# Last cross attention: the mask's bias added by VectorE for 15 of 49 pairs of key tiles

## The chip, the cores and the metric

One Trainium2 chip, one core. The metric is the device time of one execution in microseconds (us), lower is better; several runs are taken and their median is given.

## What is computed

The program is a twelve-stage network (four rounds of cross attention, self attention and feed-forward) over 128 rows of 256 features, `x`, with a context of 12544 rows of 256, `ctx_1024`. The change is in the tenth stage, the last cross attention, whose reference is this:

```python
def _L3_xattn_ref(queries, keys, values, mask):     # N_HEADS = 16
    q, k, v = heads(queries), heads(keys), heads(values)          # 16 features per head
    sim = jnp.einsum('bhqd,bhkd->bhqk', q, k) / jnp.sqrt(jnp.float32(d_head))
    bias = -1000000000.0 * (1.0 - mask.astype(sim.dtype))[:, None]
    sim = sim + bias
    weights = jax.nn.softmax(sim, axis=-1)
    out = jnp.einsum('bhqk,bhkd->bhqd', weights, v)

x = x + _L3_xattn_ref(_layernorm(x), ctx_1024, ctx_1024, mask_BxSxS2_ik1)
```

The mask has 128 x 12544 integers, 0 or 1, and is the same for all heads.

## The kernel before

`stage_l3_xattn` has 16 heads in 8 groups of two. The 12544 keys are 98 tiles of 128; two tiles are one pair, so that a group has 49 pairs and the stage 392. `SEGS` cuts the work into ten segments: group 0 in three (7, 14 and 28 pairs, so that work can begin early), each other group in one of 49. The masks' bias, `NEG` times (mask - 1), lies in SBUF for all keys as `key_bias`, rows of queries by columns of keys.

For each segment there are two passes. The first finds a maximum: TensorE multiplies queries by keys into one of two double banks `ps_s` (`scores`, L1648, two matmuls of 448 columns for a unit of 896 keys and one head), and VectorE adds the bias and reduces (`largest`, L1795). GpSimd turns the maximum of a segment into three parts that are put into the matrix of queries (`largest` of GpSimd, L1748 to L1755, which signals `m`); TensorE transposes it (`queries`, L1655), and VectorE copies it to `qb`. The second pass takes each pair of tiles with keys on the partitions (`tiles`, L1664 and L1666): for each tile a product of `key_bias` with an identity, `eye`, which lays the turned bias into PSUM, and the product of the keys with `qb`, added to it. A pair fills one of three banks `ps_t` (four tiles of 128 x 128: two tiles by two heads). ScalarE takes the exponential of the whole bank into `p` (L1727), a ring of eight. TensorE multiplies values by it (`values`, L1678).

The order on TensorE is written out: phases of four or five pairs; in each the tiles of the phase, with the scores for the next segment placed between them (`placed`: 28 units of scores and maxima over some 42 pairs, two in three pairs; none for the last group), then the values of the phase before. VectorE runs the maxima in the same order. `wait_slot` lets the tiles of a pair wait until the bank's earlier user is done, which is the exponential three pairs before, or a query or turn between. `scores` waits for the maximum two units before.

At the stage's start GpSimd clears buffers, copies the first values (`copy(0)`, L1760) and takes the first maximum (`largest(0)`). SP issues the first two loads of values, and the keys of group 1 once ScalarE has filled a buffer with ones (`k_ones`, L1722).

The core of the tiles:

```python
pe.matmul(ps_t[b][:, h * 2 * T:(h + 1) * 2 * T], bias[:, t * T:(t + 1) * T],
          eye[:, :, :].rearrange("p a t -> p (a t)"), start=True, stop=False)
mm = pe.matmul(ps_t[b][:, h * 2 * T:(h + 1) * 2 * T], kst[g % 2][:, t * T:(t + 1) * T],
               qb[:, i % 2, :, :].rearrange("p a t -> p (a t)"), start=False, stop=True)
```

Of the kernel before, what the change touches and what calls it, by code (L numbers as in the profile page):

```python
# [11 lines left out]
ALU = mybir.AluOpType  # L12
# [6 lines left out]
T = 128  # L19
# [4 lines left out]
CT = CH // 128  # L24
HALF = CH // 2
NCH = S2 // CH
ARENA = 52100
FAR = -2.0 ** 100
NEG = 954.0 * 2 ** 20
AHEAD = S2  # L30
# [1489 lines left out]
def stage_l3_xattn(nc, A, x, ident):  # L1520
# [21 lines left out]
    for i, n in enumerate(size):  # L1542
        parts = max(1, round(n / 4))
        for j in range(parts):
            phases.append((i, range(first[i] + j * n // parts, first[i] + (j + 1) * n // parts), j == parts - 1))
    fast = P * 2 * T + 2 * 2 * T + 2 * T
    with Stage(nc, "l3x", fast=fast, held=HELD) as s:
        kst, bias = A["kst"], A["key_bias"]
        qs, qb = s.sb("qs", [128, P, 2, T], F32R), s.sb("qb", [128, 2, 2, T], F32R)
# [8 lines left out]
        wide = flat("wide", P * 128).rearrange("p (g a r b) -> p g a r b", g=P, a=2, r=16)  # L1558
        v_in = flat("v_in", 2 * SEG * 32).rearrange("p (j t a e) -> p j t a e", j=2, t=SEG, a=2)
        v = flat("v", 2 * SEG * 64).rearrange("p (j t a e) -> p j t a e", j=2, t=SEG, a=2)  # L1560
        p = flat("p", R * 4 * T).rearrange("p (r j a t) -> p r j a t", r=R, j=2, a=2)
        junk = s.sb("junk", [128, 2, CH])
        qh = junk[:, 0, 0:D]
        far, negm, rest = s.sb("far", [128, 1]), s.sb("negm", [128, 2, 2]), s.sb("rest", [128, 2, 2])
# [32 lines left out]
        @block.sync  # L1597
        def _(sp):
            def keys(g, seg):
                j, lo = g % 2, seg * SEG * T  # L1600
                if g == 1:
                    sp.wait_ge(s.sem("k_ones"), seg // 4 + 1)
                for part, b in (("ctx_high", 0), ("ctx_low", 1), ("ctx_high", 2)):
                    sp.dma_start(kst[j][b:128:4, lo:lo + SEG * T].bitcast(F32),
                                 A[part][32 * g:32 * g + 32, lo:lo + SEG * T]).then_inc(s.sem(f"k_in{j}{seg}"), 16)

            def values(q):
                g, seg = divmod(q, NS)
                wait(sp, "v", q - 1)
                sp.dma_start(v_in[:, q % 2, :, :, :].rearrange("p t a e -> p (t a e)"),  # L1610
                             A["ctx_pairs"][:, g, seg * SEG * 32:(seg + 1) * SEG * 32]).then_inc(s.sem(f"v_in{q % 2}"), 16)

            values(0)
            values(1)
            for seg in range(NS):
                keys(1, seg)
            for q in range(P * NS):
                if q + 2 < P * NS:
                    values(q + 2)
                if q < (P - 2) * NS:  # L1620
                    wait(sp, "tiles", (q + 1) * 7)
                    keys(q // NS + 2, q % NS)

        @block.tensor
        def _(pe):
# [32 lines left out]
            def tiles(i, u):  # L1658
                g, b = SEGS[i][0], slot["tiles", u]
                wait_slot(pe, ("tiles", u))  # L1660
                pe.wait_ge(s.sem("qb"), 2 * i + 2)
                for h in range(2):
                    t = 2 * (u % 49) + h
                    pe.matmul(ps_t[b][:, h * 2 * T:(h + 1) * 2 * T], bias[:, t * T:(t + 1) * T],  # L1664
                              eye[:, :, :].rearrange("p a t -> p (a t)"), start=True, stop=False)
                    mm = pe.matmul(ps_t[b][:, h * 2 * T:(h + 1) * 2 * T], kst[g % 2][:, t * T:(t + 1) * T],  # L1666
                                   qb[:, i % 2, :, :].rearrange("p a t -> p (a t)"), start=False, stop=True)
                mm.then_inc(s.sem("tiles"), 1)

            def values(i, u):  # L1670
                pe.wait_ge(s.sem("v"), u // 7 + 1)
                pe.wait_ge(s.sem("p"), u + 1)
                if u == first[i]:
                    wait(pe, "outT", i)
                for h in range(2):
                    for a in range(2):
                        c = 2 * h + a
                        mm = pe.matmul(ps_o[32 * c:32 * c + 32, 0:T], v[:, u // 7 % 2, u % 7 * 2 + h, a, :], p[:, u % R, h, a, :],  # L1678
                                       start=(u == first[i]), stop=(u == first[i + 1] - 1))
                mm.then_inc(s.sem("values"), 1)  # L1680

# [28 lines left out]
        def _(act):  # L1710
# [12 lines left out]
            for i, groups, ends in phases:  # L1723
                for u in groups:
                    act.wait_ge(s.sem("tiles"), u + 1)
                    wait(act, "values", u - R + 1)
                    act.activation(p[:, u % R, :, :, :].rearrange("p h a t -> p (h a t)"), ps_t[slot["tiles", u]][:, :],  # L1727
                                   ACT.Exp).then_inc(s.sem("p"), 1)
                if accs[i] == 3 and groups[0] == first[i]:
                    act.wait_ge(s.sem("diff"), i)  # L1730
# [3 lines left out]
        def _(pool):  # L1734
# [22 lines left out]
            def copy(q):  # L1757
                pool.wait_ge(s.sem(f"v_in{q % 2}"), (q // 2 + 1) * 16)
                wait(pool, "values", (q - 1) * 7)
                pool.tensor_copy(v[:, q % 2, :, :, 0:16], v_in[:, q % 2, :, :, :]).then_inc(s.sem("v"), 1)  # L1760

            pool.wait_ge(s.sem("v_ones"), 2)
            copy(0)
            pool.wait_ge(s.sem("wide"), 1)
# [9 lines left out]
        def _(dve):  # L1774
# [32 lines left out]
            def turn(i):  # L1807
# [12 lines left out]
                dve.wait_ge(s.sem("acc"), done + accs[i] - 1)  # L1820
                dve.tensor_tensor(mine, mine, parts[:, 1, :, :], ALU.add).then_inc(s.sem("acc"), 1)

            def out(i):
                dve.wait_ge(s.sem("values"), first[i + 1])
                wait(dve, "out_ps", i)
# [5 lines left out]
            due, last = None, None  # L1831
            for i, groups, ends in phases:
                for u in groups:
                    for k in placed.get(u, []):
                        largest(k)
                if ends and i + 1 < len(SEGS):
# [1660 lines left out]
def more_layouts(i, out):  # L3497
# [11 lines left out]
    out["mask_bk1"] = i["mask_BxS2_bk1"][0].astype(np.int32)  # L3509
    out["mask_ff1"] = i["mask_BxS2_ff1"][0].reshape(-1, 128).T  # L3510
    out["mask_ik1"] = i["mask_BxSxS2_ik1"][0]
    out["L2_xattn_wq"] = chunked(i["L2_xattn_wq"])
    out["L2_xattn_wkv"] = chunked(np.concatenate([i["L2_xattn_wk"], i["L2_xattn_wv"]], 1))
    out["L2_xattn_dense_w"] = chunked(i["L2_xattn_dense_w"])
# [139 lines left out]
```

## Time and profile before

| | |
|---|---|
| median of 3 runs | 2784.79 us (2784.68 to 2785.99) |
| the profiled execution | 2784.39 us, its span 2782.7 us |
| mean granted TensorE clock | 0.949 |
| busy over the span | TensorE 2548.3 us (92%), VectorE 1637.7 (59%), ScalarE 1419.1 (51%), GpSimd 650.8 (23%) |
| the stage of the change | about 2272 to 2710 us |

The span is the time from the first to the last instruction of the profiled execution. A row of the time line has the start, the duration, the engine, the line of the code, the operation, what it writes and reads, a count of merged instructions, and in brackets how long the engine was idle before and what released it. A row of the groups has line, engine, operation, names, shapes and count, then busy time and mean of one, then the idle time before it. PE is TensorE, DVE VectorE, ACT ScalarE, POOL GpSimd, SPq the queue of SyncE. Matmuls overlap, so that their cost is the distance of their starts.

### The profile page before, as it was taken

The page shows a single profiled execution, that of the slowest core. Times are in us where ns is not written, and L with a number is a line of the kernel's source. Part 1 is how long each engine was busy: PE and PEld are TensorE (multiplying, and loading weights), DVE is VectorE, ACT ScalarE, POOL GpSimd, SP SyncE. Part 2 cuts the span into 40 slices and gives each one's busy share as a digit, 9 for nine tenths or more (in the row PEclk, how much of TensorE's full clock was granted, in tenths as well). Part 3 has the DMA queues.
Part 4 walks back from the last instruction along what each step waited for, and adds up shares of the span by engine and source line. Part 5 has one row for each costly group of instructions (what it writes and reads, how often), then busy time and mean ns, then how long its engine had stood idle before and what let it go on. Part 6 is the DMA issues. An engine that isn't in the chain of part 4 may idle for free. (4 is left out here: it accounts for less than half of the span.)

```text
span 2782.7 us, 67701 instructions
## 1 busy us (share of the span) xinstructions
PE 2548.3 (92%) x25738; PEld 2122.6 (76%) x25738; DVE 1637.7 (59%) x4181; ACT 1419.1 (51%) x2670; POOL 650.8 (23%) x888
## 2 busy tenths in 40 slices
PE   8999999999999999997859999999976359999986
PEld 6888888888888888886857888888842127888873
DVE  5667556656665566656684555555552337666625
ACT  5555555555555555553645555565520433555553
POOL 1323132313231323112014554545100000101000
PEclk9999999999999999999889999999987679999996
DMA  4011101111011101100831111112058654344310
GB/s 166 15 55 41 54 15 55 41 54 39 30 41 55 54 15 44 39 15 24 306 124 67 68 68 68 39 63 72 2 218 294 258 196 134 121 134 134 104 39 34
DMA packets 67194, 236.07 MB, mean 85 GB/s; under 512 B 12924, under 2 KB 22944, under 8 KB 60640
## 3 DMA queue, kind: packets, MB, share of 16 engines
q1 hardware_dynamic: 64208, 218.43, 22.6%
q0 software_dynamic: 2304, 8.39, 0.9%
q8 instruction: 214, 3.51, 0.5%
q10 hardware_dynamic: 368, 4.92, 0.4%
q14 instruction: 100, 0.82, 0.1%
HBM read 205.65 MB, written 26.05 MB: 83 GB/s over the span
## 5 line engine op out<-in xcount | busy, mean ns | idle before, releaser
L469 PE MATMUL l0x_psum<-l0x_fast 128*128 128x512 f32 x1764 | 432.0, 397 | 2.8 <-ACT l0x_sbuf L593 1.3
L469 PEld LDWEIGHTS l0x_psum<-l0x_fast 128*128 128x128 f32 x1764 | 323.8, 189 | 67.4 <-ACT l0x_sbuf L593 1.7
L604 ACT ACTIVATE l0x_sbuf<-l0x_sbuf 128x896 f32<-128x896 f32 x224 | 233.3, 1041 | 237.0 <-DVE l0x_sbuf L718 237.0
L1727 ACT ACTIVATE l3x_sbuf<-l3x_psum 128x512 f32<-128x512 f32 x392 | 220.9, 599 | 187.8 <-PE l3x_psum L1666 181.2
L1795 DVE CUSTOM_DVE_ANT_0 l3x_sbuf<-l3x_psum,key_bias,l3x_sbuf 128x896 f32<-128x896 f32 x224 | 249.0, 1149 | 93.3 <-PE l3x_psum L1648 76.8
L449 PE MATMUL l0x_psum<-l0x_fast 128*128 128x448 f32 x1344 | 292.5, 367 | 1.1 <-DVE l0x_fast L704 1.1
L449 PEld LDWEIGHTS l0x_psum<-l0x_fast 128*128 128x128 f32 x1344 | 252.0, 188 | 26.0 <-DVE l0x_fast L704 1.5
L718 DVE CUSTOM_DVE_ANT_0 l0x_sbuf<-l0x_psum,l0x_sbuf 128x896 f32<-128x896 f32 x224 | 249.1, 1150 | 20.6 <-PE l0x_psum L484 20.6
L855 POOL TENSOR_TENSOR l0x_sbuf<-l0x_sbuf 128x2 f32<-128x2 f32 x112 | 31.2, 278 | 890.6 <-ACT l0x_sbuf L621 890.6
L704 DVE TENSOR_TENSOR l0x_fast<-l0x_psum,l0x_fast 128x448 fp32r<-128x448 f32 x224 | 136.3, 616 | 129.3 <-ACT l0x_fast L579 129.3
L1664 PE MATMUL l3x_psum<-l3x_fast,key_bias 128*128 128x256 f32 x784 | 208.2, 296 | 0.7 <-DVE l3x_fast L1805 0.7
L579 ACT ACTIVATE l0x_fast<-l0x_psum 128x448 fp32r<-128x448 f32 x224 | 120.4, 544 | 166.3 <-PE l0x_psum L449 166.2
L1666 PE MATMUL l3x_psum<-l3x_fast,last_keys 128*128 128x256 f32 x784 | 197.1, 281 | 0.0
L529 PE MATMUL l0x_psum<-l0x_sbuf 128*32 128x128 f32 x6272 | 195.9, 274 | 1.2 <-DVE l0x_sbuf L757 1.2
L529 PEld LDWEIGHTS l0x_psum<-l0x_sbuf 128*32 128x32 f32 x6272 | 165.9, 109 | 35.1 <-issue 33.6
L704 DVE TENSOR_TENSOR l1x_fast<-l1x_psum,l1x_fast 128x448 fp32r<-128x448 f32 (+1 forms) x116 | 69.9, 612 | 207.6 <-ACT l1x_fast L579 207.3
L604 ACT ACTIVATE l1x_sbuf<-l1x_sbuf 128x896 f32<-128x896 f32 (+1 forms) x120 | 119.6, 996 | 115.1 <-DVE l1x_sbuf L718 115.1
L593 ACT ACTIVATE l0x_sbuf<-l0x_psum 128x512 f32<-128x512 f32 x196 | 117.6, 601 | 109.2 <-PE l0x_psum L469 109.2
L484 PE MATMUL l0x_psum<-l0x_fast 64*128 64x448 f32 x1344 | 167.3, 381 | 0.0
L1664 PEld LDWEIGHTS l3x_psum<-l3x_fast,key_bias 128*128 128x128 f32 x784 | 148.5, 189 | 22.6 <-issue 14.9
L966 DVE BATCH_NORM_STATS2 l0x_sbuf<-l0x_sbuf 128x6 f32<-128x256 f32 x98 | 42.0, 428 | 205.5 <-ACT l0x_sbuf L941 205.5
L741 DVE COPY l0x_sbuf<-l0x_psum 128x384 f32<-128x384 f32 x224 | 125.1, 559 | 59.1 <-PE l0x_psum L536 40.3
(767 smaller groups left out, 5153.0 us busy)
## 6 DMA issues: line engine op xcount, KB each, us to landing
ahead<-in_L_ffn_W SPq DMA_DIRECT2D x22, 1024.0 KB, 14.6
last_keys<-ctx_high SPq DMA_DIRECT2D x98, 224.0 KB, 3.5
l0x_sbuf<-in_ctxT SPq DMA_DIRECT2D x14, 896.0 KB, 6.1
l0x_sbuf<-in_ctx_rows SPq DMA_DIRECT2D x14, 896.0 KB, 4.4
ctx_high<-l0x_fast SPq DMA_DIRECT2D x14, 896.0 KB, 8.6
ctx_low<-l0x_fast SPq DMA_DIRECT2D x14, 896.0 KB, 10.2
soon<-in_ctxT SPq DMA_DIRECT2D x14, 896.0 KB, 5.0
l3x_sbuf<-in_ctx_pairs SPq DMA_DIRECT2D x56, 224.0 KB, 3.7
```

Source lines behind the costliest of these rows:

```text
L449: mm = pe.matmul(ps[:, 0:width], self.wk[w][:, c, pr * T:(pr + 1) * T], x[:, c, lo:lo + width], start=(j == 0), stop=(j == len(products) - 1))
L469: mm = pe.matmul(ps[:, :], x[:, c, t * T:(t + 1) * T], weights[w][:, c, :], start=(j == 0), stop=(j == len(products) - 1))
L484: mm = pe.matmul(self.ps_s[a][:, i, 0:width], self.q[q][half, pr, :], self.k[k][half, m % 2, lo:lo + width], start=(j == 0), stop=(j == 2))
L529: mm = pe.matmul(self.ps_o[32 * c:32 * c + 32, :], self.v[:, m // 4 % 2, t, at:at + 32], self.pT[:, (2 * m + c // 2) % 4, t, :], start=(t ...
L604: act.activation(self.p[:, (2 * m + a) % 4, 0:width], self.sm[:, a, 0:width], ACT.Exp, scale=-1.0, bias=self.negm[:, n % 2, 2 * pr + a:2 * ...
L704: dve.tensor_tensor(self.k[1][:, m % 2, lo:lo + width], self.ps_kv[self.slot["k", m, i]][:, 0:width], self.k[0][:, m % 2, lo:lo + width].b ...
L718: dve.tensor_tensor_reduce(self.sm[:, a, 0:parts * width].rearrange("p (i c) -> p i c", i=parts), self.ps_s[a][:, 0:parts, 0:width], bias. ...
L741: dve.tensor_copy(self.pT[:, i % 4, 4:CT, :], cols(self.turned_banks(m, a)[1], CT - 4)).then_inc(s.sem(f"ptb{a}"), 1)
L1664: pe.matmul(ps_t[b][:, h * 2 * T:(h + 1) * 2 * T], bias[:, t * T:(t + 1) * T], eye[:, :, :].rearrange("p a t -> p (a t)"), start=True, sto ...
L1666: mm = pe.matmul(ps_t[b][:, h * 2 * T:(h + 1) * 2 * T], kst[g % 2][:, t * T:(t + 1) * T], qb[:, i % 2, :, :].rearrange("p a t -> p (a t)") ...
L1727: act.activation(p[:, u % R, :, :, :].rearrange("p h a t -> p (h a t)"), ps_t[slot["tiles", u]][:, :], ACT.Exp).then_inc(s.sem("p"), 1)
L1795: dve.tensor_tensor_reduce(junk[:, a, :].rearrange("p (i c) -> p i c", i=2), ps_s[a][:, :, 0:HALF], bias[:, n * CH:(n + 1) * CH].bitcast(F ...
```

## The change

Of the 49 pairs of a group, the 15 with numbers 2, 5, 8, ..., 44 are masked on VectorE in all eight groups, 120 pairs in all. For these TensorE leaves out the two products with the identity; VectorE adds `-NEG * outside` to the bank in PSUM (one SCALAR_TENSOR_TENSOR over 128 x 512, in place), where `outside` is 1 - mask as bytes with keys on the partitions, the same bytes for both heads. ScalarE waits for it before the exponential. The host hands in the turned mask of these pairs as integers (`mask_turned`, 128 x 15 x 2 x 128, 1.97 MB). SP loads it into the space of `p`, and GpSimd turns it into bytes before its first copy. The order inside a bank and inside a slot of `p` changes from tile, head to head, tile, so that one broadcast serves both heads.

```diff
-ARENA = 52100
+ARENA = 52148
+    apart = {u: i for i, u in enumerate(range(2, 47, 3))}
+    set_apart = [u for u in range(P * 49) if u % 49 in apart]
+    masked = {u: i + 1 for i, u in enumerate(set_apart)}
-        p = flat("p", R * 4 * T).rearrange("p (r j a t) -> p r j a t", r=R, j=2, a=2)
+        p = flat("p", R * 4 * T).rearrange("p (r a j t) -> p r a j t", r=R, a=2, j=2)
+        outside = s.sb("outside", [128, len(apart) * 2 * T // 4], I32).bitcast(mybir.dt.uint8).rearrange(
+            "p (u h t) -> p u h t", u=len(apart), h=2)
+        raw = p[:, :, :, :, :].rearrange("p r a j t -> p (r a j t)").bitcast(I32)[:, 0:len(apart) * 2 * T].rearrange(
+            "p (u h t) -> p u h t", u=len(apart), h=2)
             values(1)
+            sp.dma_start(raw, A["mask_turned"]).then_inc(s.sem("turned_in"), 16)
             for seg in range(NS):
...
                     t = 2 * (u % 49) + h
-                    pe.matmul(ps_t[b][:, h * 2 * T:(h + 1) * 2 * T], bias[:, t * T:(t + 1) * T],
-                              eye[:, :, :].rearrange("p a t -> p (a t)"), start=True, stop=False)
-                    mm = pe.matmul(ps_t[b][:, h * 2 * T:(h + 1) * 2 * T], kst[g % 2][:, t * T:(t + 1) * T],
-                                   qb[:, i % 2, :, :].rearrange("p a t -> p (a t)"), start=False, stop=True)
+                    both = ps_t[b][:, :].rearrange("p (a h t) -> p a h t", a=2, h=2)[:, :, h, :]
+                    if u not in masked:
+                        pe.matmul(both, bias[:, t * T:(t + 1) * T],
+                                  eye[:, :, :], start=True, stop=False)
+                    mm = pe.matmul(both, kst[g % 2][:, t * T:(t + 1) * T], qb[:, i % 2, :, :], start=u in masked, stop=True)
...
                     wait(act, "values", u - R + 1)
+                    if u == 0:
+                        act.wait_ge(s.sem("outside"), 1)
+                    if u in masked:
+                        act.wait_ge(s.sem("masked"), masked[u])
...
+            pool.wait_ge(s.sem("turned_in"), 16)
+            pool.tensor_scalar(outside, raw, -1.0, 1.0, ALU.mult, ALU.add).then_inc(s.sem("outside"), 1)
             pool.wait_ge(s.sem("v_ones"), 2)
             copy(0)
...
+            def mask(u):
+                dve.wait_ge(s.sem("outside"), 1)
+                dve.wait_ge(s.sem("tiles"), u + 1)
+                both = ps_t[slot["tiles", u]][:, :].rearrange("p (a k) -> p a k", a=2)
+                dve.scalar_tensor_tensor(out=both, in0=outside[:, apart[u % 49], :, :].rearrange("p h t -> p (h t)").unsqueeze(1).to_broadcast([128, 2, 2 * T]),
+                                         scalar=-NEG, in1=both, op0=ALU.mult, op1=ALU.add).then_inc(s.sem("masked"), 1)
...
                 for u in groups:
+                    if u in masked:
+                        mask(u)
                     for k in placed.get(u, []):
                         largest(k)
```

## Rows read from the trace of the kernel before

**Rows 1.** Stretches of the stage: busy time by engine, granted clock, DMA share, GB/s.

```profile
core 0: us, PE busy (x) PEld busy (x) DVE busy (x) ACT busy (x) POOL busy (x), PEclk, DMA share, GB/s
...
2292.00:2305.30 13.30, 10.47 (x69) 8.36 (x69) 9.23 (x18) 7.37 (x9) 1.60 (x7) 0.88 0.95 329
2305.30:2329.70 24.40, 21.07 (x202) 17.63 (x202) 18.64 (x37) 8.36 (x15) 2.17 (x8) 0.92 0.34 114
2329.70:2370.00 40.30, 37.71 (x402) 30.99 (x398) 31.94 (x62) 16.76 (x29) 2.67 (x8) 0.97 0.29 91
...
2419.40:2468.70 49.30, 49.30 (x650) 43.50 (x646) 32.65 (x61) 27.73 (x50) 4.68 (x12) 1.00 0.43 132
...
2666.20:2705.50 39.30, 39.26 (x633) 35.19 (x629) 0.74 (x3) 25.61 (x50) 3.75 (x7) 1.00 0.12 32
```

**Rows 2.** Groups of instructions of the stage, 2292 to 2706 us.

```profile
L1795 DVE CUSTOM_DVE_ANT_0 l3x_sbuf<-l3x_psum,key_bias,l3x_sbuf 128x896 f32<-128x896 f32 x220 | 244.6, 1149 | 88.1 <-PE l3x_psum L1648 71.6 <-issue 16.5
...
L1664 PE MATMUL l3x_psum<-l3x_fast,key_bias 128*128 128x256 f32 x784 | 208.2, 296 | 0.7 <-DVE l3x_fast L1805 0.7
...
L1648 PE MATMUL l3x_psum<-last_keys,l3x_fast 128*128 128x448 f32 x440 | 128.4, 376 | 3.2 <-DVE l3x_sbuf L1795 3.1
```

**Rows 3.** Time line inside a full round, all engines.

```profile
2400.22 0.57 PE L1648 MATMUL l3x_psum<-last_keys,l3x_fast 128*128 128x448 f32 x2
2400.42 0.60 ACT L1727 ACTIVATE l3x_sbuf<-l3x_psum 128x512 f32<-128x512 f32 x1 [1.46 <-PE l3x_psum L1666]
...
2400.62 0.28 PE L1664 MATMUL l3x_psum<-l3x_fast,key_bias 128*128 128x256 f32 x1
...
2400.83 1.15 DVE L1795 CUSTOM_DVE_ANT_0 l3x_sbuf<-l3x_psum,key_bias,l3x_sbuf 128x896 f32<-128x896 f32 x1 [0.92 <-PE l3x_psum L1648]
...
2401.09 0.28 PE L1664 MATMUL l3x_psum<-l3x_fast,key_bias 128*128 128x256 f32 x1
...
2402.44 0.57 PE L1648 MATMUL l3x_psum<-last_keys,l3x_fast 128*128 128x448 f32 x2
...
2402.94 1.08 PE L1678 MATMUL l3x_psum<-l3x_sbuf 128*32 128x128 f32 x32
...
2403.95 0.38 PE L1664 MATMUL l3x_psum<-l3x_fast,key_bias 128*128 128x256 f32 x1
...
2404.17 0.28 PE L1666 MATMUL l3x_psum<-l3x_fast,last_keys 128*128 128x256 f32 x1
```

**Rows 4.** Time line of maxima and scores among pairs 21 to 48.

```profile
2348.95 1.15 DVE L1795 CUSTOM_DVE_ANT_0 l3x_sbuf<-l3x_psum,key_bias,l3x_sbuf 128x896 f32<-128x896 f32 x1 [0.78 <-PE l3x_psum L1648]
...
2350.03 1.15 DVE L1795 CUSTOM_DVE_ANT_0 l3x_sbuf<-l3x_psum,key_bias,l3x_sbuf 128x896 f32<-128x896 f32 x1
...
2350.26 0.65 PE L1648 MATMUL l3x_psum<-last_keys,l3x_fast 128*128 128x448 f32 x2
```

**Rows 5.** Time line at the end of a round: ScalarE's exponentials, TensorE's next tile.

```profile
2416.43 2.07 ACT L1727 ACTIVATE l3x_sbuf<-l3x_psum 128x512 f32<-128x512 f32 x4 [1.04 <-PE l3x_psum L1666]
...
2417.17 0.30 PE L1664 MATMUL l3x_psum<-l3x_fast,key_bias 128*128 128x256 f32 x1
```

**Rows 6.** Groups of VectorE over the whole span, shapes kept apart.

```profile
L3077 DVE SCALAR_TENSOR_TENSOR l0f_sbuf<-l0f_sbuf,l0f_psum 128x512 f32<-128x512 f32 x16 | 10.4, 685 | 21.9 <-ACT l0f_sbuf L3044 21.9
```

**Rows 7.** Time line of the stage's start: SP and GpSimd.

```profile
2272.33 0.80 SPq L1610 DMA_DIRECT2D l3x_sbuf<-in_ctx_pairs  x2
...
2277.55 0.56 POOL L1760 COPY l3x_sbuf<-l3x_sbuf 128x448 f32<-128x448 f32 x1
...
2289.47 0.19 POOL L1748 CAST l3x_sbuf<-l3x_sbuf 128x2 fp32r<-128x2 f32 x1 [11.37 <-DVE l3x_sbuf L1795]
...
2289.65 0.49 SPq L1604 DMA_DIRECT2D last_keys<-ctx_high  x1
```

**Rows 8.** Groups of GpSimd over the whole span, shapes kept apart.

```profile
L828 POOL TENSOR_SCALAR l1x_sbuf<-l1x_sbuf 128x896 f32<-128x896 int32 x14 | 45.2, 3226 | 29.4 <-DMA l1x_sbuf<-in_mask_bk 28.3
...
L809 POOL TENSOR_SCALAR soon<-soon,l1x_sbuf 128x896 f32<-128x896 f32 x26 | 28.4, 1092 | 2.7
```

More of the change, by code:

```diff
@@ L1677, in values @@
                         c = 2 * h + a
-                        mm = pe.matmul(ps_o[32 * c:32 * c + 32, 0:T], v[:, u // 7 % 2, u % 7 * 2 + h, a, :], p[:, u % R, h, a, :],
+                        mm = pe.matmul(ps_o[32 * c:32 * c + 32, 0:T], v[:, u // 7 % 2, u % 7 * 2 + h, a, :], p[:, u % R, a, h, :],
                                        start=(u == first[i]), stop=(u == first[i + 1] - 1))
@@ L1726, in _ @@
                     wait(act, "values", u - R + 1)
-                    act.activation(p[:, u % R, :, :, :].rearrange("p h a t -> p (h a t)"), ps_t[slot["tiles", u]][:, :],
+                    if u == 0:
+                        act.wait_ge(s.sem("outside"), 1)
+                    if u in masked:
+                        act.wait_ge(s.sem("masked"), masked[u])
+                    act.activation(p[:, u % R, :, :, :].rearrange("p a h t -> p (a h t)"), ps_t[slot["tiles", u]][:, :],
                                    ACT.Exp).then_inc(s.sem("p"), 1)
@@ L3511, in more_layouts @@
     out["mask_ik1"] = i["mask_BxSxS2_ik1"][0]
+    out["mask_turned"] = i["mask_BxSxS2_ik1"][0].T.reshape(49, 2, 128, T)[2:47:3].transpose(2, 0, 1, 3)
     out["L2_xattn_wq"] = chunked(i["L2_xattn_wq"])
```

## The prediction

> **What bounds the kernel now.** I read the stage of the last cross attention by stretches first [rows 1]. Its columns give, for each stretch, the busy time of every engine and the granted clock. From 2370 us on the 392 pairs of key tiles run in rounds of 49 pairs. A full round (2419.40 to 2468.70) has TensorE busy all 49.30 us at clock 1.00, VectorE 32.65 and ScalarE 27.73. So TensorE sets the pace of the six rounds that also compute scores for the next one, and of the last round (39.26 of 39.30 us, VectorE only 0.74). The first 49 pairs are different: TensorE 10.47 of 13.30, 21.07 of 24.40 and 37.71 of 40.30 us, clock 0.88 to 0.97. There scores and maxima come more densely, and the stage starts.
>
> Next the groups of the stage [rows 2]. The product with the identity, L1664, runs 784 times, two for each pair. Its mean of 296 ns is latency, since matmuls overlap. What a matmul costs must be read from the distance of starts [rows 3]: two score matmuls (one "S") take 2400.22 to 2400.62, 0.40 us. A pair has four tile matmuls; 2400.62 to 2401.09 are four of them, so T = 0.47 us, 0.117 each. A pair without identity is T' = 0.23 us. After a phase of four pairs come the 32 value matmuls "V": 2402.94 to 2403.95, and with 0.10 ahead of it 1.11 us. The first tile matmul after V takes 0.22 in place of 0.12 (2403.95 to 2404.17).
>
> **The sum for TensorE alone.** Twelve pairs (three phases) have 8 S: 12 x 0.47 + 8 x 0.40 + 3 x (1.11 + 0.10) = 12.5 us. A round of 49 pairs in 49.3 us fits that. The change takes out 2 x 120 = 240 of these matmuls, 30 per round: 30 x 0.117 = 3.5 us per round, 28 in all. That is the most it can bring. From 12.5 a cycle of twelve pairs would fall to 11.6.
>
> **The new path.** In a masked pair ScalarE's exp no longer follows the product directly. VectorE must add the bias first, in its own order, behind the maxima that it has queued. Behind the waiting mask stand the next maxima (L1795) and so TensorE's next scores. Behind the exp that waits stand all later exps. A pair uses one of three PSUM banks, so the tiles of pair u+3 wait for the exp of pair u.
>
> The prices. A maximum occupies VectorE for 1.15 us, but the next starts 1.07 to 1.08 later [rows 2, 4]. A first maximum starts 0.61 after its S starts (2400.22 to 2400.83), an exp 0.20 after the last tile matmul has been issued (2400.22 to 2400.42) [rows 3]. S waits for the maximum two before it, plus 0.23 (2350.03 to 2350.26) [rows 4]. Exp runs 0.60 us, back to back every 0.49, and TensorE goes on 0.14 after the end of it (2416.43 + 0.60 to 2417.17) [rows 3, 5]. For the mask M no row writes PSUM from VectorE. The nearest is a SCALAR_TENSOR_TENSOR of 128x512 with one operand in PSUM, 685 ns [rows 6]. I take M = 0.68. The lower bound is one element at the pace of the 896-element maximum, 512/896 x 1.15 = 0.66; the upper one is the whole price of that maximum, 1.15. Bytes as input I price like fp32. With 0.1 from VectorE to ScalarE the bank of a masked pair is free 0.84 us after M ends.
>
> **One cycle by hand**, time 0 at the first tile after V. TensorE: T0 0, S0 0.57, T1, S1 1.44, T2' ends 2.07, T3, S3 2.54, V, T4 4.05, S4 4.62, T5', T6, S6 5.72, T7, S7 6.59, V, T8' 8.10, T9, S9 8.91, T10, S10 9.78, T11' 10.18, V, end 11.52. VectorE: maxima 1.18, 2.25; M2 3.32 to 4.00; maxima 4.00, 5.23; M5 6.30 to 6.98; maxima 6.98, 8.05; M8 9.12 to 9.80; maxima 9.80, 10.87; M11 11.94 to 12.62; the next may start at 12.70. VectorE's sum is 8 x 1.07 + 4 x 0.68 = 11.3 of 11.5 us, so it just keeps up and is always late by about a maximum. Which banks are late? Pair 6 needs exp 3, which queued behind exp 2: 0.08. Pair 11 needs the bank of pair 8: 9.80 + 0.84 = 10.64 against 10.18: 0.46. The others are in time, mostly because V stands between. A cycle gains 0.93 - 0.54 = 0.39.
>
> The rest of a round: pairs 36 to 39 gain 0.23. In the last nine pairs two masks save 0.47, but pair 44 waits 0.52 for the mask of 41, and pair 47 waits for 44 with only two pairs between them: 0.21 + 0.68 + 0.84 = 1.73 less 2 x 0.47 is 0.79. That is 0.84 lost. A round gains 3 x 0.39 + 0.23 - 0.84 = 0.56, six rounds 3.4 us. In the last round 15 x 0.23 = 3.5 are saved and four times 0.79 lost (8 to 11, 20 to 23, 32 to 35, 44 to 47): 0.3.
>
> **The first 49 pairs.** Pairs 0 to 6 run eight maxima without a gap, then GpSimd takes the result. M2 stands among them: +0.7; M5 comes after them and is hidden. Pairs 7 to 20 have 16 maxima and VectorE 18.64 of 24.40 us busy [rows 1]; four masks are 2.7 us, and V's gaps can take some 1.5 of it: +1.2. In pairs 21 to 48 each V leaves a gap of 0.78 in front of a maximum [rows 4]. One mask fits in, and eight masks meet seven phases, one of them saved matmuls too: +0.3. Together +2.2, bounds 0.5 and 8 (no cover for twelve of the masks).
>
> **The start.** GpSimd now waits for 1.97 MB of mask, turns it to bytes, and only then does copy and `largest(0)`, for which the first `m`, the queries, every tile and every maximum wait. Before, that chain began at 2289.47, its cover since the copy of 2277.55 [rows 7]. The issue follows the two at 2272.33, so at 2273.1. At 329 GB/s with the DMA 0.95 busy [rows 1], 1.97 MB take 6 us; with 0.45 MB ahead and some 1.5 us to land, about 2281.4. Then the pass of 3840 integers a partition. The nearest row is a TENSOR_SCALAR from int32 on GpSimd: 896 elements in 3226 ns [rows 8], 3.5 ns each above 0.1, so 13.4 us. The same instruction on fp32 takes 1092 ns, which would be 4.7 us. The integer row shares the input type, so I take it: end 2294.8, copy 0.6, `largest(0)` at 2295.5 in place of 2289.5: +6.0. Nothing takes this back, since the first pairs are VectorE's. Bounds 0 and 10. The added DMA issue on SP stands ahead of the loads of the next keys, which wait for ScalarE's fill until 2289.65 anyway [rows 7]: nothing. The layout of `p` and of the PSUM bank leaves all counts and sizes as they were: nothing, bounds -1 and +1.
>
> The Trainium skill speaks against my price for the pass: "GPSIMD Engine Reference", section 4.1 Engine selection, says that one-input elementwise work on GpSimd is roughly at line rate. By it the pass would be hidden (first rival). The fp32 row agrees with it, the int32 row does not.
>
> **Sum.** +6.0 + 2.2 - 3.4 - 0.3 = +4.5 us on the profiled execution's 2784.39 (span 2782.7 and 1.7 around it), which is 0.4 under the median of 2784.79: 2789.3. A measurement here tells about 0.2% (5.6 us) from no change, so this lies just inside "same".
>
> **Rivals.**
> 1. Quick bytes: the pass runs at the fp32 row's 1.2 ns, is done by 2286 and hidden. Time 2783. For it the fp32 row, against it the int32 row, 14 times alike. Its rule is the one of the page named above.
> 2. Masks hidden: VectorE's real lateness is smaller than I drew, because its handover is shorter or the order slips into V. Then most of 3.5 us per round stays: half of it gives 2784.4 + 6 + 2 - 14 = 2778, all of it 2766. For it: TensorE has no slack today and VectorE has 16 us idle per round. Against it: two pairs between 44 and 47, 8 and 11.
> 3. VectorE becomes the bound (slower). Place: the cycle of twelve pairs. It decides from M = (12.5 - 8.6)/4 = 0.98 us on; writing PSUM or reading bytes would have to cost 0.3 more than the 685 ns row. At 0.98 a cycle gains nothing and the tails lose 0.3 more for each late bank: 2784.4 + 6 + 5 + 6 x 1.5 + 1.5 = 2806; at 1.15 about 2820.
> 4. Bytes out cost extra on GpSimd: 5 ns per element, 19 us, start +12: 2795. No row writes bytes, so nothing excludes it.
> 5. The change does not do what it says (the identity products stay): 2790.
>
> **Chances.** Forecast 0.45 (own range 2784 to 2795), rival 1 0.15, 2 0.13, 3 0.13, 4 0.12, 5 0.02. Faster: rival 2, and 0.02 each of the forecast and rival 1, 0.17. Slower (above 2790.4): 0.17 of the forecast, rivals 3 and 4, 0.42. Within: the rest, 0.41. The range for 8 in 10 leaves out the far ends of rivals 2 and 3: 2779 to 2804.
>
> **What will show it.** L1664 has 544 matmuls. GpSimd's TENSOR_SCALAR to uint8 x1 lasts 13.4 us (4.7: rival 1; 19: rival 4), and the cast of `largest(0)` starts near 2295.5. The masks x120 show 0.68 us. A full round takes 48.8 us; TensorE has gaps of some 0.5 before pair 11 and 0.8 before pair 47 of a round, released by ScalarE. If a round takes 46 to 47 us, rival 2 holds; if VectorE is busy throughout and a round exceeds 50, rival 3. The clock stays 1.00 in the rounds; a lower one there would make the prediction wrong in a way that I have not priced.

## The result and the profile after

The changed kernel takes 2790.3 us (median of 20 runs, 2783.15 to 2795.76), the kernel before 2786.05 in the same runs. The ratio is 1.0019, with a 95% interval of 1.0012 to 1.0026: 5 us slower (3 to 7), within the 0.2% that the prediction called "same". The forecast was 2789.3.

The profiled execution took 2785.99 us (span 2784.2), one of the quicker ones. Executions of one and the same code differ by a few us, so the change is read from the stage alone, and there from its parts. The table cuts the stage at the start of the first load on SP, at the first cast of each set of queries on VectorE, and at the first load of the next stage. All numbers are us from the traces; the kernels below the second row are the experiments of the next section.

| kernel | start | pairs 0-6 | 7-20 | 21-48 | a full round | six rounds | last round | stage |
|---|---|---|---|---|---|---|---|---|
| before | 18.96 | 13.28 | 24.40 | 40.36 | 49.36 | 295.94 | 44.71 | 437.65 |
| after | 18.67 | 13.88 | 25.40 | 41.59 | 49.05 | 294.20 | 47.49 | 441.23 |
| setup_only | 18.67 | 13.40 | 23.56 | 39.02 | 49.54 | 297.03 | 44.64 | 436.32 |
| layout_only | 18.95 | 13.28 | 24.23 | 39.85 | 49.36 | 295.95 | 44.69 | 436.95 |
| no_add | 18.67 | 13.70 | 24.83 | 38.57 | 46.07 | 276.18 | 43.02 | 414.97 |
| both | 18.66 | 13.93 | 25.60 | 41.85 | 51.43 | 308.32 | 49.30 | 457.66 |
| first_only | 18.67 | 14.15 | 25.07 | 41.73 | 49.54 | 297.03 | 44.64 | 441.29 |
| rounds_only | 18.67 | 13.28 | 24.24 | 39.82 | 49.05 | 294.10 | 44.64 | 434.75 |
| one_a_phase | 18.67 | 13.28 | 24.22 | 39.82 | 48.30 | 289.59 | 44.65 | 430.23 |
| no_tail | 18.67 | 13.73 | 23.73 | 40.71 | 48.20 | 288.98 | 44.65 | 430.47 |
| without_5 | 18.67 | 13.43 | 23.57 | 39.01 | 48.51 | 291.08 | 44.62 | 430.38 |
| best | 18.66 | 13.28 | 24.30 | 39.94 | 47.73 | 286.17 | 43.94 | 426.29 |

The six rounds of a trace repeat within 0.1 us, save the first, which is some 0.2 us shorter in most traces ("a full round" is one of the other five). The first 49 pairs vary from kernel to kernel: seven other kernels mask nothing there, and with before they take 76.0 to 78.2 us for the same work.

Stretches of after, the columns as in [rows 1]: the three segments of the first 49 pairs, a full round, and 12.5 us of the last round (some fifteen pairs).

```profile
2289.45:2303.36 13.91, 10.29 (x65) 8.17 (x66) 10.45 (x20) 7.35 (x9) 1.61 (x7) 0.87 0.96 331
2303.36:2328.76 25.40, 20.30 (x188) 16.11 (x188) 21.52 (x42) 7.92 (x15) 2.18 (x8) 0.90 0.31 105
2328.76:2370.30 41.54, 35.77 (x390) 28.93 (x384) 36.61 (x70) 15.86 (x29) 2.69 (x8) 0.98 0.28 84
2418.50:2467.50 49.00, 47.70 (x620) 40.27 (x620) 41.13 (x76) 25.96 (x50) 4.82 (x11) 1.00 0.43 133
...
2676.30:2688.80 12.50, 11.88 (x181) 9.80 (x180) 3.48 (x5) 8.57 (x16) 1.14 (x2) 1.00 0.14 39
```

In a full round VectorE rose from 32.65 to 41.13 us, TensorE is no longer busy throughout (47.70 of 49.00), and the clock stayed at 1.00. In the last round TensorE has gaps too. In the first 49 pairs VectorE is busy 85 to 88% of the second and third segment.

The groups of the stage in after: the mask on VectorE, the identity product, the exponential.

```profile
L1842 DVE SCALAR_TENSOR_TENSOR l3x_psum<-l3x_sbuf,l3x_psum 128x512 f32<-128x512 uint8 x120 | 83.2, 693 | 33.7 <-PE l3x_psum L1676 33.1
...
L1674 PE MATMUL l3x_psum<-l3x_fast,key_bias 128*128 128x256 f32 x544 | 151.8, 303 | 3.7 <-ACT l3x_sbuf L1740 3.0
...
L1740 ACT ACTIVATE l3x_sbuf<-l3x_psum 128x512 f32<-128x512 f32 x392 | 210.1, 599 | 202.5 <-DVE l3x_psum L1842 149.9
```

The change does what it says: 544 identity products in place of 784, 120 masks at 693 ns. The exponential's idle time is now mostly ended by the mask.

And the start of the stage, time line of SP and GpSimd.

```profile
2270.08 0.81 SPq L1617 DMA_DIRECT2D l3x_sbuf<-in_ctx_pairs  x2
2270.93 0.42 SPq L1622 DMA_DIRECT2D l3x_sbuf<-in_mask_turned  x1
...
2280.59 3.39 POOL L1776 TENSOR_SCALAR l3x_sbuf<-l3x_sbuf 128x3840 uint8<-128x3840 int32 x1 [5.36 <-DMA l3x_sbuf<-in_mask_turned]
...
2286.93 0.19 POOL L1761 CAST l3x_sbuf<-l3x_sbuf 128x2 fp32r<-128x2 f32 x1 [2.43 <-DVE l3x_sbuf L1810]
```

The load lands 9.6 us after its issue, the pass takes 3.39 us and not 13.4, and GpSimd waits another 2.43 us for VectorE before the cast of `largest(0)`, 16.85 us after the first issue of the stage (2270.08). In the trace of before it is 17.14 [rows 7]. So the start costs nothing.

### The profile page after: what moved, and what is told of

Read it like the earlier page. It is cut to its first block and busy times, and to the rows that moved or that the text cites. A ratio compares the mean times of both kernels' runs of the same rounds, so it can differ in the third digit from the quotient of the medians.

```text
span 2784.2 us, 67470 instructions
## 1 busy us (share of the span) xinstructions
PE 2526.9 (91%) x25498; PEld 2088.9 (75%) x25498; DVE 1713.8 (62%) x4301; ACT 1408.4 (51%) x2670; POOL 655.5 (24%) x889
## 3 DMA queue, kind: packets, MB, share of 16 engines
q8 instruction: 212, 3.47, 0.5%
## 5 line engine op out<-in xcount | busy, mean ns | idle before, releaser
L1740 ACT ACTIVATE l3x_sbuf<-l3x_psum 128x512 f32<-128x512 f32 x392 | 210.1, 599 | 202.5 <-DVE l3x_psum L1842 149.9
L1676 PE MATMUL l3x_psum<-l3x_fast,last_keys 128*128 128x256 f32 x784 | 191.0, 290 | 4.0 <-ACT l3x_sbuf L1740 3.6
L1676 PEld LDWEIGHTS l3x_psum<-l3x_fast,last_keys 128*128 128x128 f32 x784 | 143.5, 190 | 20.1 <-ACT l3x_sbuf L1740 14.6
L1674 PE MATMUL l3x_psum<-l3x_fast,key_bias 128*128 128x256 f32 x544 | 151.8, 303 | 3.7 <-ACT l3x_sbuf L1740 3.0
```

The lines of the kernel that those rows point to most:

```text
L1674: pe.matmul(both, bias[:, t * T:(t + 1) * T], eye[:, :, :], start=True, stop=False)
L1676: mm = pe.matmul(both, kst[g % 2][:, t * T:(t + 1) * T], qb[:, i % 2, :, :], start=u in masked, stop=True)
L1740: act.activation(p[:, u % R, :, :, :].rearrange("p a h t -> p (a h t)"), ps_t[slot["tiles", u]][:, :], ACT.Exp).then_inc(s.sem("p"), 1)
```

## The experiments

The theory to begin with was the prediction's, less its start: TensorE's saving is full where it sets the pace, and is eaten by PSUM banks that the mask's detour over VectorE frees late. Rivals were that the loss comes from the load, the layout or the larger stage; that TensorE would not have gained in the first place; and, for cures, that the number of masks counts and not their place.

**setup_only**: the load, the bytes and the layout, no pair masked.

```diff
-    set_apart = [u for u in range(P * 49) if u % 49 in apart]
+    set_apart = []
```

> The mask is loaded and turned to bytes at the stage's start, the new layout is used, but no pair is masked on VectorE: all identity products stay. Prediction's step (the pass costs 13.4 us and delays the first tiles by 6.0): time before + 6, so ratio 1.002. First rival (the pass takes 3.4 us as the trace of after shows, and lies in GpSimd's wait): time before, ratio 1.000, first cast of the queries 18.7 to 19.0 us after the stage's first load is issued, rounds of 49.36 us.

Measured: 2784.26 us, ratio 0.9995 (0.9986 to 1.0004); start 18.67 us. The prediction's +6.0 falls, the first rival's picture of the start holds. The full rounds are 49.54 us, 0.18 longer than in before, which neither expected.

**layout_only**: the kernel before, with the order of bank and slot changed.

```diff
...
+                    both = ps_t[b][:, :].rearrange("p (a h t) -> p a h t", a=2, h=2)[:, :, h, :]
-                    pe.matmul(ps_t[b][:, h * 2 * T:(h + 1) * 2 * T], bias[:, t * T:(t + 1) * T],
-                              eye[:, :, :].rearrange("p a t -> p (a t)"), start=True, stop=False)
+                    pe.matmul(both, bias[:, t * T:(t + 1) * T], eye[:, :, :], start=True, stop=False)
...
```

> The kernel before with only the order inside bank and slot changed (head, tile in place of tile, head): no load, no bytes, no mask. setup_only showed rounds of 49.54 in place of 49.36 us. If the layout costs this, rounds are 49.54 here; if the load, the larger stage or the bytes do, 49.36.

Measured: rounds of 49.36 us, one run of 2786.62. The layout costs nothing: TensorE writes two stretches of 128 columns, 256 apart, as quickly as 256 in a row. The Trainium skill, "PSUM — Partial Sum Buffer", Specifications, says that any non-contiguous pattern slows matmuls significantly; for stretches this long the measurement says no. The 0.18 of setup_only must then come from the rest of the set-up: the load, the bytes, the waits that go with them or the 48 words by which the stages' arena grew; which one was not tried. It is no single wait: from one group of value products to the next setup_only takes 4.33, 4.32 and 3.91 us in a cycle of twelve pairs, layout_only 4.30, 4.30 and 3.92.

**no_add**: the saving alone. VectorE's addition and ScalarE's wait for it are left out, so that the masked keys of these pairs are counted in.

```diff
-                    if u in masked:
-                        act.wait_ge(s.sem("masked"), masked[u])
...
-                    if u in masked:
-                        mask(u)
```

> The identity products of the 120 pairs are left out and VectorE adds nothing, so that the masked keys of these pairs are counted in: what is left is TensorE's saving alone. If the handover through VectorE is what eats the gain (prediction), the six full rounds fall by 3.3 to 3.5 us each, 20 us together; the first 49 pairs stay, since maxima set their pace (0 to 2 us). For the last round two theories: by the prediction's sum it falls by 3.5 us; if three banks and the exponential bound its phases (a bank is free 0.9 us after its tile, two tiles are 0.94), only masked pairs at the first or last place of a phase save, about 2 us. Total: 22 to 25 us under before, ratio 0.992. If TensorE had not been the bound: ratio 1.000.

Measured: 2759.75 us, ratio 0.9906 (0.9891 to 0.9921). Against setup_only a full round falls by 3.47 us (49.54 to 46.07), which is all of 30 x 0.117 = 3.5. The last round falls by 1.62 only: the theory of three banks and the exponential said 2, the prediction's sum 3.5. The first 49 pairs take 77.1 us, no less than without the change: VectorE's maxima set their pace.

**both**: the detour alone. The 120 pairs keep their identity products and are masked by VectorE as well.

```diff
-                    if u not in masked:
+                    if True:
...
-                    mm = pe.matmul(both, kst[g % 2][:, t * T:(t + 1) * T], qb[:, i % 2, :, :], start=u in masked, stop=True)
+                    mm = pe.matmul(both, kst[g % 2][:, t * T:(t + 1) * T], qb[:, i % 2, :, :], start=False, stop=True)
```

> The 120 pairs keep their identity product and get VectorE's addition as well (the masked scores are lowered twice, which leaves their exponential at zero): the handover alone. Prediction: full rounds of 12 pairs rise from 12.5 by some 0.3, the last nine pairs of a round by 1.3 to 1.5, so a round is 51 to 51.5 us; the last round gains 4 to 6 us; the first 49 pairs rise by 3 to 4. Total 15 to 22 us over before, ratio 1.006 to 1.008. Rival (the wait is hidden and the loss in after has another source, such as the load or the layout): ratio under 1.002.

Measured: 2806.93 us, ratio 1.0077 (1.0063 to 1.0091). Against setup_only a round rises by 1.9, the last round by 4.7, the first 49 pairs by 5.4 (by 4.2 against the mean of the kernels without masks there). The detour is dear by itself, and saving and detour do not simply add up: per round -3.47 + 1.89 is -1.6, while after shows -0.49. The likely reading of the other 1.1 us is saving that turns into waiting, since with shorter tiles TensorE reaches a late bank sooner; the gaps below show such waits.

**first_only**: the masks of group 0 alone.

```diff
-    set_apart = [u for u in range(P * 49) if u % 49 in apart]
+    set_apart = [u for u in range(49) if u % 49 in apart]
```

> Only the 15 masked pairs of group 0 (the first 49 pairs) go over VectorE, all others keep the identity product. By the trace of after these three segments cost 0.6 + 1.0 + 1.2 = 2.8 us, since VectorE's maxima set their pace: ratio 1.001. The prediction had 2.2. Rival (the loss there is noise of one execution): ratio 1.000 and the three segments within 0.3 us of before.

Measured: 2788.53 us, ratio 1.0014 (1.0005 to 1.0023). Segments 14.15, 25.07 and 41.73: together 80.95, as in after (80.87). The eight kernels without masks there (before, setup_only, layout_only, rounds_only, one_a_phase, no_tail, without_5, best) have a mean of 13.37, 24.03 and 39.82; against it the mean of after and first_only (14.02, 25.24, 41.66) is a loss of 0.6, 1.2 and 1.8 us.

**rounds_only**: the masks of the six rounds alone.

```diff
+    set_apart = [u for u in range(49, 343) if u % 49 in apart]
```

> Masked pairs only in the six rounds that also compute scores (pairs 49 to 342, 90 of them). By the parts read from after: six rounds 1.7 us under before, the rest as before: ratio 0.9994. Rival (the parts of the stage pull on each other, so that the loss of the first 49 pairs comes back elsewhere): ratio 1.001 or more.

Measured: 2780.49 us, ratio 0.9989 (0.9980 to 0.9997). Rounds of 49.05, first 49 pairs 77.3, last round 44.64: the parts do not pull on each other.

**Where a round loses.** In the second round of after, the time line marks three waits of TensorE. Around the first of them, all engines (the first row is TensorE's):

```profile
2426.34 0.57 PE L1656 MATMUL l3x_psum<-last_keys,l3x_fast 128*128 128x448 f32 x2
...
2426.03 0.69 DVE L1842 SCALAR_TENSOR_TENSOR l3x_psum<-l3x_sbuf,l3x_psum 128x512 f32<-128x512 uint8 x1
...
2426.84 1.58 ACT L1740 ACTIVATE l3x_sbuf<-l3x_psum 128x512 f32<-128x512 f32 x3 [1.65 <-DVE l3x_psum L1842]
...
2427.49 0.33 PE L1695 MATMUL l3x_psum<-ident,l3x_sbuf 128*128 128x128 f32 x1 [0.58 <-ACT l3x_sbuf L1740]
2427.75 1.08 PE L1687 MATMUL l3x_psum<-l3x_sbuf 128*32 128x128 f32 x32
```

The mask of pair 5 ends at 2426.72, its exponential runs 2426.84 to 2427.44, and only then may the turn of the round before (L1695, the transposition of its sums, which takes a bank of the same ring) have the bank. The bracket counts from the modelled end of a matmul that overlaps the next, so the whole cost is read from the starts: two score matmuls take 0.40 us [rows 3], here the turn starts 1.15 after them, which is a wait of 0.75. The other two waits, 0.28 and 0.35 in brackets, lie before pairs 44 and 47. Below are the same two of the round before. Their brackets say 0.28 and 0.36; by the starts they are 0.36 (1.37 in place of 1.01 from values to tile) and 0.51 (0.63 in place of 0.12):

```profile
2413.66 1.08 PE L1687 MATMUL l3x_psum<-l3x_sbuf 128*32 128x128 f32 x32
...
2414.37 1.58 ACT L1740 ACTIVATE l3x_sbuf<-l3x_psum 128x512 f32<-128x512 f32 x3 [1.44 <-PE l3x_psum L1687]
2415.03 0.51 PE L1676 MATMUL l3x_psum<-l3x_fast,last_keys 128*128 128x256 f32 x2 [0.28 <-ACT l3x_sbuf L1740]
...
2415.64 0.70 DVE L1842 SCALAR_TENSOR_TENSOR l3x_psum<-l3x_sbuf,l3x_psum 128x512 f32<-128x512 uint8 x1 [1.38 <-PE l3x_psum L1676]
...
2416.45 2.07 ACT L1740 ACTIVATE l3x_sbuf<-l3x_psum 128x512 f32<-128x512 f32 x4 [0.50 <-DVE l3x_psum L1842]
...
2416.47 0.28 PE L1676 MATMUL l3x_psum<-l3x_fast,last_keys 128*128 128x256 f32 x1
2417.10 0.38 PE L1674 MATMUL l3x_psum<-l3x_fast,key_bias 128*128 128x256 f32 x1 [0.36 <-ACT l3x_sbuf L1740]
```

Shorter waits carry no bracket. Before pair 23, whose bank pair 20 had, the scores take 0.60 and not 0.40, and the pair's two products another 0.44 up to the values, where 0.33 is the least:

```profile
2442.23 0.57 PE L1656 MATMUL l3x_psum<-last_keys,l3x_fast 128*128 128x448 f32 x2
2442.83 0.51 PE L1676 MATMUL l3x_psum<-l3x_fast,last_keys 128*128 128x256 f32 x2
2443.27 1.08 PE L1687 MATMUL l3x_psum<-l3x_sbuf 128*32 128x128 f32 x32
```

Together 0.31, and the same before pair 35.

From that came four kernels with other choices of masked pairs; the first three mask pairs in the six rounds alone.

**one_a_phase**:

```diff
+    set_apart = [u for u in range(49, 343) if u % 49 in (2, 5, 11, 14, 17, 23, 26, 29, 35, 38)]
```

> Masked pairs only in the six rounds, and there ten of them (2, 5, 11, 14, 17, 23, 26, 29, 35, 38): none in the last nine pairs, none of the pairs 8, 20 and 32 whose bank is wanted again within one phase. If a bank that is wanted again within the phase is what eats the saving, each of the ten keeps its 0.23 us: 2.0 to 2.3 us a round, 12 to 14 in all, ratio 0.9955. If VectorE's total load is what counts, it keeps only as much as the fewer masks cost: a round gains about 0.6, ratio 0.9987.

Measured: 2777.89 us, ratio 0.9977 (0.9968 to 0.9986), rounds of 48.30. That is 1.24 under setup_only, between the two theories. Twelve pairs take 11.94 us with three masks (3.67, 4.18, 4.09 by phase), 0.62 less than the 12.56 of setup_only, so nearly all of 0.70 is kept, where four masks (no_tail 11.99) keep 0.57 of 0.93. Inside the cycle the three masks keep nearly all of their gain. What is missing in the round is the turn's wait, still there (1.15 from scores to turn, 0.75 too much).

**no_tail**:

```diff
+    set_apart = [u for u in range(49, 343) if u % 49 in apart and u % 49 < 40]
```

> As the 15 of 49 in the six rounds, but without pairs 41 and 44 (13 a round). By the trace of after a cycle of twelve pairs takes 12.00 in place of 12.52, so three cycles give 1.56 and pair 38 another 0.23: 1.8 us a round, 11 in all, ratio 0.996. If the tail is not where a round loses, it stays at 0.3 a round, ratio 0.9994.

Measured: 2776.3 us, ratio 0.9967 (0.9955 to 0.9979), rounds of 48.20. Two masks less make a round 0.85 us shorter than in rounds_only. It is also 0.10 shorter than in one_a_phase, though pairs 8, 20 and 32 are masked again: by phases pair 8 gains 0.15, and pairs 20 and 32 cost some 0.05 each. So a bank that is wanted again within the phase hardly matters here; the tail and the turn do. The expected 1.8 us under before was 1.16: the turn still waits.

**without_5**:

```diff
+    set_apart = [u for u in range(49, 343) if u % 49 in apart and u % 49 != 5]
```

> The six rounds with 14 masked pairs, only pair 5 left out. If the turn waits for the bank of pair 5, its wait of 0.58 us before the transposition is gone and a round falls from 49.06 to 48.7 us. If it waits for something else (the copy of the sums, the values), the wait stays and a round rises to 49.3.

Measured: 2776.82 us (one run), rounds of 48.51 us, 0.54 under rounds_only, and no idle time before the turn. It was the bank of pair 5. The 0.54 is more than the expected 0.36 because the wait was 0.75 by the starts and not the bracket's 0.58: 0.75 - 0.23 = 0.52.

**best**: nine pairs in a round, three in the last round.

```diff
+    set_apart = [u for u in range(49, 343) if u % 49 in (2, 11, 14, 17, 23, 26, 29, 35, 38)]
+    set_apart += [u for u in range(343, 392) if u % 49 in (11, 23, 35)]
```

> Masked pairs only where no bank is wanted while the mask is on its way: in the six rounds 2, 11, 14, 17, 23, 26, 29, 35, 38 (pair 5 is out, since the turn of the round before takes its bank and waits 0.58 us for it), in the last round 11, 23, 35 (last place of a phase, values follow). Theory of the bank's next user: a round loses 0.58 of waiting and 0.23 of saving against one_a_phase, so it is 48.30 - 0.35 = 47.95 us; the last round 44.65 - 0.7 = 43.95. Together 2.8 us under one_a_phase, about 2775, ratio 0.9967. Rival (the number of masks counts, not the place): rounds of 48.4, last round 44.6 or more, ratio 0.998.

Measured: 2773.51 us (2770.88 to 2776.21, 5 runs), ratio to before 0.9959 (0.9945 to 0.9972): 11 us faster than before and about 17 faster than after (each against before in its own runs). VectorE's first cast of two rounds:

```profile
2464.59 0.28 DVE L1820 CAST l3x_fast<-l3x_psum 64x128 fp32r<-64x128 f32 x1 [3.97 <-PE l3x_psum L1664]
...
2512.33 0.28 DVE L1820 CAST l3x_fast<-l3x_psum 64x128 fp32r<-64x128 f32 x1 [3.98 <-PE l3x_psum L1664]
```

A round is 47.74 us (expected 47.95), the last round 43.94 (43.95). The 0.2 below the expected round is again the turn's 0.75 in place of 0.58. 57 masks in chosen places bring what 120 in even spacing do not; that no choice is better was not tried (pair 8 is left out, and brought 0.15 in no_tail).

**micro** and **micro2**: single instructions, one after another, nothing of the network. The edit is a stage of its own; these are its forms on GpSimd, three times over in micro (the last four in micro2 alone):

```diff
+                link(pool.tensor_scalar(by[:, 0:3840], raw[:, :], -1.0, 1.0, ALU.mult, ALU.add))
...
+                link(pool.tensor_scalar(g[:, 0:896], raw[:, 0:896], -1.0, 1.0, ALU.mult, ALU.add))
+                link(pool.tensor_scalar(g[:, 0:896], raw[:, 0:896], 1.0, -FAR, ALU.subtract, ALU.mult))
+                link(pool.tensor_scalar(g[:, 0:896], f[:, 0:896], -1.0, 1.0, ALU.mult, ALU.add))
+                link(pool.tensor_scalar(g[:, 0:896], f[:, 0:896], 1.0, -FAR, ALU.subtract, ALU.mult))
...
+                link(pool.tensor_scalar(g[:, 0:896], f[:, 0:896], 1.0, 2.0, ALU.subtract, ALU.mult))
+                link(pool.tensor_scalar(g[:, 0:896], f[:, 0:896], -1.0, -FAR, ALU.add, ALU.mult))
+                link(pool.tensor_scalar(g[:, 0:896], f[:, 0:896], -FAR, FAR, ALU.mult, ALU.add))
+                link(pool.tensor_scalar(g[:, 0:896], f[:, 0:896], 1.0, None, ALU.subtract))
```

> Single instructions, one after another, nothing of the network: GpSimd's TENSOR_SCALAR with int32 in and bytes or fp32 out, 3840 and 896 elements, operations (multiply, add) and (subtract, multiply); VectorE's SCALAR_TENSOR_TENSOR 128x512 with bytes or fp32 in, out to PSUM or SBUF. Prediction's theory (int32 as input is slow): all int32 forms cost 3.5 ns an element. Rival a (the pair of operations with the large constant is slow): only (subtract, multiply) on int32 takes 3.2 us for 896. Rival b (the output type): only fp32 out is slow and bytes out takes 0.9 ns. Rival c (the neighbours): all forms take about 0.9 ns here, and the 3.2 us came from what ran beside it. VectorE: all forms within 20 ns of 690.

> As micro, with more forms of GpSimd's TENSOR_SCALAR on 896 fp32 elements: (subtract 1, multiply 2), (add -1, multiply 2^100), (multiply 2^100, add -2^100) and subtract alone. If the operation subtract is what costs 3.2 us, the first and the last form take 3.2 and the others 0.94. If it is the large constant, the second and third take 3.2. If only the order (multiply, add) is quick, the second takes 3.2 and the third 0.94 as well as, perhaps, the last.

Time line of GpSimd in micro: bytes from int32, 3840 elements; fp32 from int32, 896; the same with (subtract, multiply); then both pairs of operations on fp32.

```profile
11.99 3.39 POOL L3618 TENSOR_SCALAR mic_sbuf<-mic_sbuf 128x3840 uint8<-128x3840 int32 x1
...
19.96 0.94 POOL L3621 TENSOR_SCALAR mic_sbuf<-mic_sbuf 128x896 f32<-128x896 int32 x1
20.98 3.21 POOL L3622 TENSOR_SCALAR mic_sbuf<-mic_sbuf 128x896 f32<-128x896 int32 x1
24.28 0.94 POOL L3623 TENSOR_SCALAR mic_sbuf<-mic_sbuf 128x896 f32<-128x896 f32 x1
25.30 3.20 POOL L3624 TENSOR_SCALAR mic_sbuf<-mic_sbuf 128x896 f32<-128x896 f32 x1
```

In micro2 the four further forms, in the order of the edit:

```profile
28.41 3.20 POOL L3625 TENSOR_SCALAR mic_sbuf<-mic_sbuf 128x896 f32<-128x896 f32 x1
31.70 0.94 POOL L3626 TENSOR_SCALAR mic_sbuf<-mic_sbuf 128x896 f32<-128x896 f32 x1
32.72 0.94 POOL L3627 TENSOR_SCALAR mic_sbuf<-mic_sbuf 128x896 f32<-128x896 f32 x1
33.74 2.46 POOL L3628 TENSOR_SCALAR mic_sbuf<-mic_sbuf 128x896 f32<-128x896 f32 x1
```

Neither the integer input, nor the output (3840 elements take 3.39 us as bytes and as fp32), nor the large constant, nor the order costs anything, and no work on other engines runs beside it here: the operation subtract is what costs. With it 896 elements take 3.20 us, alone 2.46; without it 0.94.

VectorE in micro: the mask's form, bytes in and PSUM out, then the same from PSUM to SBUF, then with fp32 in place of bytes.

```profile
62.44 0.70 DVE L3640 SCALAR_TENSOR_TENSOR mic_psum<-mic_sbuf,mic_psum 128x512 f32<-128x512 uint8 x1
63.17 0.69 DVE L3640 SCALAR_TENSOR_TENSOR mic_sbuf<-mic_sbuf,mic_psum 128x512 f32<-128x512 uint8 x1
63.89 0.69 DVE L3640 SCALAR_TENSOR_TENSOR mic_psum<-mic_sbuf,mic_psum 128x512 f32<-128x512 f32 x1
```

## Why the prediction was right in its time and wrong in its parts

The total, 2789.3 against 2790.3, is right by luck: one step was 6 us too high, and three together about as much too low.

- **The start, +6.0: wrong, measured -0.3.** The failed step is the choice of the row for the pass, "the integer row shares the input type, so I take it". The row of [rows 8] shares the type and differs in the operation: L828 is (subtract, multiply), the pass is (multiply, add), as L809 is. micro shows 0.94 us for 896 integers by the latter. The first rival held here: 3840 elements in 3.39 us is 0.88 ns each. The Trainium skill, "GPSIMD Engine Reference", section 4.1 Engine selection, says that one-input work is roughly at line rate, and the pass agrees with its 0.88 ns an element; (subtract, multiply), at 3.20 us for 896, does not. Rival 1 was thus right in its mechanism, and its total of 2783 was missed by the losses below. Rival 4 (bytes out are dear) falls by micro, rival 5 by the 544 identity products. The landing was estimated within 1.3 us (8.3 after the issue, measured 9.6).
- **The mask's price, 0.68: right.** 693 ns, and writing PSUM or reading bytes adds 0.01 at most in micro (685 in [rows 6]). The next maximum starts 0.60 after it (2294.74 to 2295.34 in after), 0.08 earlier than drawn. Rival 3 never came near its 0.98.
- **The cycle of twelve pairs: right in kind.** Forecast 12.06 by the same sum that gave 12.45 before, so -0.39; measured 12.00 against 12.52, -0.52. The wait it drew before the last pair of the cycle (0.46) is there, at pairs 23 and 35, with 0.31; before pair 11 only some 0.08 of it shows.
- **The last nine pairs: right.** The loss was put at 0.84. Their phases are 0.25 and 0.63 us longer than before, 0.88 in all. By the starts the two waits are 0.36 and 0.51 where I had 0.52 and 0.79. What makes up for it is that the masked pairs save less than 0.23 here: behind pairs 41 and 44 and behind the late bank the next product takes 0.20 to 0.22 and not 0.12 in this trace, so that the first of the two phases saves 0.11 and the second nothing.
- **The turn: missing from the sum.** The prediction listed the tiles' claims on banks and left out that a turn takes one as well, the bank of pair 5, and waits for its exponential: 0.75 a round by the starts (0.58 in the bracket), 4.5 us in all. The cycles gave back 0.13 each more than drawn. So a round gained 0.31 and not 0.56 (six rounds 1.7 in place of 3.4).
- **The last round, -0.3: wrong, measured +2.8.** The failed step is "15 x 0.23 are saved". Without scores, the two pairs between two uses of a bank take 2 x 0.47 = 0.94 us on TensorE, and the exponential frees it after about 0.9 (0.20 to its start, 0.60, and 0.05 to 0.14 on): TensorE arrives just as it comes free. With a masked pair between, 0.94 becomes 0.70, and the rest is waiting, so a masked pair in the middle of a phase saves nothing. The row of three products at 2676.33 shows it: the next starts after 0.50 in place of 0.36, and takes 0.22 in place of 0.12, together 0.24, all of the 0.23 saved. In no_add, without any detour, the same three take 0.50 too. In before a phase takes 3.11 (first two rows), in after it is 3.11, 3.11 and, where a masked pair's bank is wanted in the same phase, 3.52:

```profile
2672.72 0.39 PE L1664 MATMUL l3x_psum<-l3x_fast,key_bias 128*128 128x256 f32 x1
...
2675.83 0.39 PE L1664 MATMUL l3x_psum<-l3x_fast,key_bias 128*128 128x256 f32 x1
```

```profile
2675.40 0.39 PE L1674 MATMUL l3x_psum<-l3x_fast,key_bias 128*128 128x256 f32 x1
...
2676.33 0.51 PE L1676 MATMUL l3x_psum<-l3x_fast,last_keys 128*128 128x256 f32 x3
2676.83 0.39 PE L1674 MATMUL l3x_psum<-l3x_fast,key_bias 128*128 128x256 f32 x1
2677.05 0.28 PE L1676 MATMUL l3x_psum<-l3x_fast,last_keys 128*128 128x256 f32 x1
...
2678.51 0.39 PE L1674 MATMUL l3x_psum<-l3x_fast,key_bias 128*128 128x256 f32 x1
...
2681.62 0.50 PE L1676 MATMUL l3x_psum<-l3x_fast,last_keys 128*128 128x256 f32 x2
...
2683.69 0.50 PE L1676 MATMUL l3x_psum<-l3x_fast,last_keys 128*128 128x256 f32 x2 [0.62 <-ACT l3x_sbuf L1740]
...
2685.14 0.39 PE L1674 MATMUL l3x_psum<-l3x_fast,key_bias 128*128 128x256 f32 x1
```

no_add confirms that only part was to be had (1.62 of 3.5), and best that a mask in the last place of a phase keeps its gain: three masks, -0.7.
- **The first 49 pairs, +2.2: mechanism right, size short.** Measured 0.6, 1.2 and 1.8 against 0.7, 1.2 and 0.3. The third term was mis-sized. It let gaps of 0.78 take all but one of eight masks. In the trace of before VectorE's gaps before a maximum in pairs 21 to 48 are six, four of 0.78 or 0.79 and two of 0.33 and 0.57, 4.0 us together; in after 0.7 is left. They take 3.3 of the masks' 4.8 us (8 x 0.60), and 1.5 lengthens the work of VectorE, which sets the pace.
- **Rival 2** (the masks hidden): no. ("All of it" would be 2764 by its own terms, 2784.4 + 8 - 28, and not 2766.) no_add shows that 3.5 us a round were there, and both that the detour takes back 1.9 by itself; with the shorter tiles it takes more.

The sum with measured terms: -0.3 (start) + 3.7 (first 49 pairs, after alone: 80.9 against 77.2) - 1.7 (rounds) + 2.8 (last round) = 4.5 us on the stage, against 4 to 5 us between the medians. What stays open: which part of the set-up makes a round 0.18 us longer in some kernels (after's gain of 0.31 a round already bears it), and why the first 49 pairs vary by 2 us between executions.

## What to carry to other kernels

Work moved from a full engine to an idle one pays by what it does to the buffer between them: a bank that takes a detour is late for its next user, so put the detour where that user is far off (here where the values' matmuls stand between), and count every user of the ring, the rare ones too. Check stretch by stretch who sets the pace before crediting a saving: all 120 masks cost 5 us, 57 of them in chosen places brought 11. Where instructions overlap, read a wait from the distance of starts, since the bracket is too small. And when a row serves as a price, match its operation before its type.

## What the hardware showed that was not expected

GpSimd's TENSOR_SCALAR on 128x896 takes 0.94 us with (multiply, add) and 3.20 us with (subtract, multiply), on int32 and fp32 alike. On fp32 (add, multiply) takes 0.94 as well and subtract alone 2.46; those two were not run on int32. There, writing -1 as an addend in place of subtracting 1 makes the same instruction 3.4 times as quick. TensorE wrote two stretches of 128 columns a product, apart in a bank, at no cost (rounds of 49.36 us either way).
